# Constant products on TensorE in the waits of a token tower's block stages

## The reference

```python
h = _L0_tok_ref(x, ...)
h = h + _L0_attn_ref(_layernorm(h), ...)   # softmax attention over 64 tokens, a norm over the whole batch, relu
h = h + _L0_ffn_ref(_layernorm(h), ...)    # rmsnorm, 4-head attention with rotary tables, rmsnorm, 8 gated experts, 2 chosen
h = h + _L1_attn_ref(_layernorm(h), ...)   # norm, softmax attention with relative bias, norm
h = h + _L1_ffn_ref(_layernorm(h), ...)    # gelu hidden layer, softmax router, 1 of 8 experts
h = h + _L2_attn_ref(_layernorm(h), ...)   # linear attention with two softmaxes, norm, gelu mlp
h = h + _L2_ffn_ref(_layernorm(h), ...)    # shared mlp and 4 relu experts, 2 chosen
h = h + _L3_attn_ref(_layernorm(h), ...)   # sigmoid attention with 8 heads
h = h + _L3_ffn_ref(_layernorm(h), ...)    # top 2 of 8 gelu experts
```

## Time and profile before

| | us |
|---|---|
| median of three runs | 8839.58 (8835.07 to 8847.66) |
| the profiled execution, its own time | 8844.81 |
| its span, first to last instruction | 8843.0 |
| tokenizer, up to the load of the weights | 5853 |
| first loop (`l0a`), eight iterations | 5875 to 6073 |
| second loop (eight stages), eight iterations | 6100 to 8843 |

### The profile page before, as it was taken

One profiled execution on the slowest core, in us unless ns is written; L12 is line 12 of the kernel. 1 busy time (PEld: TensorE's weight loads), 2 busy tenths in 40 slices (PEclk: granted clock), 3 DMA queues, 4 the chain that ended last, 5 costly groups with the idle time before them and its releaser, 6 DMA issues. The chain is left out here.

```text
span 8843.0 us, 127696 instructions
## 1 busy us (share of the span) xinstructions
PE 7317.0 (83%) x40310; PEld 3642.9 (41%) x40310; DVE 5728.9 (65%) x11559; ACT 2224.5 (25%) x3750; POOL 31.1 (0%) x35
## 2 busy tenths in 40 slices
PE   6888886999999699999879999965666766767667
PEld 5544444544444644444452222223333333333333
DVE  4799995688888478888747777755454454454453
ACT  3222122211111211111132222223333333333333
POOL 0000000000000000000000000000000000000000
PEclk8999998999999899999989999976777777778788
DMA  7655557666666866666684444420000000000000
GB/s 214 136 126 121 126 126 182 193 178 180 181 181 181 219 170 181 181 180 179 169 218 118 122 123 118 117 83 5 1 2 3 1 3 3 1 3 3 1 3 2
DMA packets 641754, 957.80 MB, mean 108 GB/s; under 512 B 527640, under 2 KB 531296, under 8 KB 582758
## 3 DMA queue, kind: packets, MB, share of 16 engines
q1 hardware_dynamic: 641416, 953.52, 40.8%
HBM read 621.97 MB, written 344.28 MB: 109 GB/s over the span
## 5 line engine op out<-in xcount | busy, mean ns | idle before, releaser
L603 PE MATMUL abank<-inv_basis,mode_tile 128*128 128x512 f32 x2048 | 1023.9, 624 | 172.6 <-DMA mode_tile<-m_modes 161.8
L970 DVE TENSOR_TENSOR work<-inv_copy,abank 128x512 f32<-128x512 f32 x1024 | 657.2, 683 | 613.9 <-ACT inv_copy L845 613.5
L665 PEld LDWEIGHTS gbank<-fwd_basis,turned 128*128 128x128 f32 x6368 | 747.1, 193 | 369.8 <-issue 221.5
L665 PE MATMUL gbank<-fwd_basis,turned 128*128 128x128 f32 x6368 | 823.0, 283 | 51.3 <-ACT turned L853 51.3
L1001 DVE TENSOR_TENSOR arena<-zbank,work 128x512 f32<-128x512 f32 x1024 | 701.6, 685 | 207.5 <-PE zbank L638 207.4
L634 PE MATMUL zbank<-arena,conv_bd 128*64 128x512 f32 x3072 | 829.2, 618 | 3.1 <-DVE mixed L1159 2.2
L636 PE MATMUL zbank<-arena,conv_bd 128*64 128x504 f32 x3072 | 779.6, 586 | 0.0
L638 PE MATMUL zbank<-arena,conv_bd 128*64 128x504 f32 x3072 | 779.6, 586 | 0.0
L1003 DVE SCALAR_TENSOR_TENSOR arena<-arena 128x512 f32<-128x512 f32 x1024 | 708.5, 692 | 35.4
L853 ACT ACTIVATE turned<-tbank 128x512 f32<-128x512 f32 x796 | 432.0, 594 | 1100.5 <-PE tbank L652 1100.5
L603 PEld LDWEIGHTS abank<-inv_basis,mode_tile 128*128 128x128 f32 x2048 | 365.4, 196 | 543.6 <-issue 495.4
(11 more groups left out here) (302 smaller groups left out, 9180.3 us busy)
## 6 DMA issues: line engine op xcount, KB each, us to landing
h_rows<-arena SPq DMA_DIRECT2D x192, 1024.0 KB, 16.3
arena<-h_rows SPq DMA_DIRECT2D x192, 1024.0 KB, 6.2
arena<-h_rows SPq DMA_DIRECT2D x384, 496.0 KB, 8.9
m_modes<-mixed SPq DMA_DIRECT2D x64, 1024.0 KB, 6.7
mode_tile<-m_modes SPq DMA_DIRECT2D x512, 128.0 KB, 4.3
g_modes<-modes_out SPq DMA_DIRECT2D x192, 256.0 KB
arena<-x_slots SPq DMA_DIRECT2D x192, 194.9 KB
arena<-g_modes SPq DMA_DIRECT2D x36, 1024.0 KB, 11.0
```

The costliest lines, as they stand in the source:

```text
L603: last = nc.tensor.matmul(abank[px][:], mode_tile[u][:, 2 * px + k, :, :].rearrange("p a c -> p (a c)"), inv[:, 2 * px + k, :], start=True ...
L665: last = nc.tensor.matmul(gbank[u][:, 128 * k:128 * k + 128], turned[q][:, k // 2, k % 2, b, :], fwd[:, 2 * q + b, k, :], start=(q == 0 an ...
L970: nc.vector.tensor_tensor(inverse[:, 2 * k + part, :], inv_copy[k][:], abank[1][:], op)\
```

## The change

A helper `fill(n, bank)` issues n products of constants: stationary operand `cst[:, 0:128]`, moving operand `cst[:, 0:512]`, into a whole PSUM bank that is free at that place. No semaphore is counted by them and nobody reads the bank before it is written again. Thirteen places in TensorE's program call it, 11 products in each iteration of the first loop and 108 in each iteration of the second. Nothing is removed or moved.

```diff
+        def fill(n, bank):
+            for _ in range(n):
+                mm(bank[:], cst[:, 0:128], cst[:, 0:512])
...
 (attn_tensor, behind the scores, ahead of the softmax's transposes; l0a and l1a)
+            fill(11, B[0][1])
             p.need("dve", "p", 1)
...
         def l0b_tensor(p):
+            fill(3, B[0][1])
...
         def l0f_tensor(p):
+            fill(6, B[0][1])
             halves_tensor(p, "r", r, "r.out")
...
                     if k == 0:
+                        if u == 0:
+                            p.need("dve", "masked0", 0)
+                            fill(20, B[0][0])
                         p.need("dve", "p", u)
...
+            fill(4, B[0][2])
             halves_tensor(p, "f", r, "f.out")
...
+            fill(11, B[0][0])
             for u in R:
                 p.need("dve", "gates", u)
...
         def l1a_tensor(p):
+            fill(6, B[0][0])
...
         def l1f_tensor(p):
+            fill(16, B[0][1])
...
         def l2a_tensor(p):
+            fill(6, B[0][2])
...
+            fill(6, B[1][2])
             stacked_tensor(p, "f", "f.out")
...
         def l2f_tensor(p):
+            fill(7, B[0][0])
...
         def l3a_tensor(p):
+            fill(6, B[0][0])
...
         def l3f_tensor(p):
+            fill(6, B[0][0])
```

## The result

The changed kernel takes 8877.17 us (median of 6 runs, 8862.20 to 8898.57) against 8840.92 (6 runs, 8835.07 to 8850.27) of the kernel before: ratio 1.004, interval 1.0026 to 1.0054, or 36 us slower. The sign is as forecast, and the time lies in the range, but the loss is 36 us where 79 were forecast.

A forecast was written before the change was run, and what follows sets the result against it. The kernel was taken as bound by one chain passing between engines, none near full, with TensorE's clock low in waits. Lateness 26.5 plus slow starts 7.5 less faster work 26, with the first loop, gave +79 us: 8918, range 8825 to 9010.

The forecast's parts named there:

- The sign: Whole kernel: slower, forecast 0.9%; slower had chance 0.74, same 0.12, faster 0.14.
- term 3: Second loop: slow work between the waits becomes fast, 63 us of it at 0.41, saving 26 us per iteration.
- term 2: Second loop: fills that begin at the low clock lose 2.5 us at three places, 7.5 us per iteration.
- the line for `l0b`: Ahead of `l0b` in the second loop: fill of 2.6 us against a wait of 4.7, so not late.
- term 1: Second loop: fills longer than their waits make TensorE late, 26.5 us per iteration, none of it hidden.
- The price of a product: Every fill: one product is two records, 0.86 us at clock 1.00 and about 1.75 us at 0.50.
- rival D: All fills: a product costs a quarter of the rows' price, none is late; about 8615 us, chance 0.04.
- The sum: Second loop: 26.5 + 7.5 - 26 = +8 us per iteration, +64 in eight; with the first loop +79.
- The first loop's term: First loop: fill of 11 late by 3.7 us, about 1.8 given back; +1.9 per iteration, +15 in eight.
- Rival B: Second loop: clock high everywhere, no fill begins slow, 34 us of work saved; about 8780 us, chance 0.12.
- Rival C: Second loop: clock falls between fill and work, all twelve late fills begin slow; about 9095 us, chance 0.08.

The follow-up runs named there:

- no_head: The changed kernel without its fill of 3 products ahead of `l0b`, the other twelve fills as they are; 8882.88 us, 1.0048 of the kernel before.
- head_moved: The changed kernel with the 3 products ahead of `l0b` put at the end of `l3f`, in front of the loop's jump; 8888.61 us, 1.005 of the kernel before.
- fine: The changed kernel with products of 256 columns, their numbers fitted to the waits, none at `l0b`; 8652.08 us, 0.9784 of the kernel before.
- thin: The changed kernel with all fill products on 8 rows of the array instead of 128; 9724.34 us, 1.0998 of the kernel before.
- fit: The changed kernel with each full-width fill cut to the 0.86 us products that fit its wait, none at `l0b`; 8671.42 us, 0.98 of the kernel before.
- part runs: The kernel before with only the 20 products in the softmax of `l0f` (8897.08 us), or only the 47 at six openings behind `x_stacked` (8800.55 us).
- plus: The fitted full-width fills with one product more at every place, two at the softmax of `l0f`; 8686.33 us, 0.9826 of the kernel before.
- heated: The fitted full-width fills, 3 at the first norm of `l0f`, plus a few products in short waits where the clock still fell; 8649.59 us, 0.9781 of before.
- softmax_only: The kernel before with only the 20 products in the softmax of `l0f` added; 8897.08 us, 1.0058 of the kernel before.

## Why the prediction was right, and where not

The sign and the mechanism held: late fills cost about as much as the clock returns. The size did not, 36 us instead of 79. What failed are three terms of the second loop's sum: term 3, which counted 63 us of work that becomes fast where it was 85.4; term 2, 7.5 us where 2.6 came; and the line for `l0b` in term 1, "not late", which was late by 3.8.

**The price of a product: right.** 0.86 us at 1.00 and 1.75 at 0.50. Twelve records take 5.4 us (5.2 were forecast), none of such groups 2.6, and rival D fell with it.

**Term 1, +26.5 us: right.** The fills that run at 1.00 have the lengths forecast: 9.5 at the router and in `l1a`, 3.3 at the second norm, 5.0 at `l2a` and `l3f`, 13.6 at `l1f`.

**Term 2, +7.5 us: too large by 4.9.** The places where the wait is longer than term 1 makes it are the softmax of `l0f` (18.6 against 17.2), the start of `l1a` (6.6 against 5.2) and some fills of `l3a` (5.7 against 5.2 on average), together 3.4 us. Net of the fast fills, up to 0.2 us shorter than 0.86 times their number, it is 32.9 - 26.5 - 3.8 = 2.6 us. The first norm's fill, one of the three that I took as slow, isn't: it stands behind the three products of `l0b`, and no_head shows that they are the reason (5.2 us with them, 7.4 without). The clock that my step read from a row of the kernel before was changed by the fill ahead of it.

**`l0b`, "2.6 against 4.7, not late": this step failed.** It is late by 3.8 us. I compared a fast fill with the wait and saw in the wait only a wait for ScalarE. In the changed kernel's row TensorE begins 3.61 us after its last work, with no engine to wait for, and then works three products slowly. The same jump is there before too, under a wait for ScalarE that is longer than the pause:

```profile
6783.07 0.63 PE L1616 MATMUL banks<-constants,pT 128*128 128x128 f32 x4 [0.85 <-ACT pT L2761]
6788.33 1.27 PE L1816 MATMUL banks<-constants,qt 64*128 64x64 f32 x8 [4.63 <-ACT qt L1810]
```

That the jump is what takes the 3.6 us is argued from its place (it is there once in each iteration, and absent where a fill stands elsewhere); that it can be hidden by products queued ahead of it is shown by head_moved.

**Term 3, -26 us: too small by 4.9.** The work gained 30.9. The step took 81 us of slow time in the work before, left 18 of them slow, and priced the other 63 at 0.41. By the table the slow time in the work is 99.2 before and 13.8 after, so 85.4 us went, and they brought 30.9, 0.36 each. What was sized wrong is how many of them go, and most of that is the 81. I took nine tenths of the long waits as slow, 62 of 68.5 us, with the softmax wait of `l0f` as the only one read. By the trace of the kernel before it is 48.5: 2.5 of the 6.1 us at the softmax of `l1a`, 0.6 of the 4.5 at `l2f`. The slow time that isn't there lies in the work. Of the two stretches that I left slow, the sums of `l1f` became fast (the slow part of `l1f`'s work fell from 17.5 to 3.4) and the end of `l2f` stayed slow as I had it (17.6 to 7.5).

**The sum.** Together -4.9, -4.9 and +3.8: +2.0 us an iteration instead of +8, and 11 us in the whole second loop instead of 64. The first loop's term was right, 18 us for 15. That gives 29 us in place of 79. The profiled executions are only 17 apart because that of the changed kernel reached the first loop 11.6 us earlier, in code that is the same. The 7 us between 29 and the 36 of the medians are within the spread of the six runs, 36 us.

**Rival B** had half of the mechanism: the clock is 0.97, near to everywhere high. It was to save 34 us of work; 31 came. What it left out are `l0b` and the slow starts that remain, together 6.4 us, and those put the result on the slower side. The Trainium skill's advice against idle gaps between bursts of products ("TensorE: Matmul & The Clock Gate", section "Why this matters for your kernels") agrees with the traces as far as the clock goes, 0.79 to 0.97. It says nothing of what a filled gap may cost, and that decided the time here: 8877 us with the gaps overfilled, 8652 with the same gaps but that of `l0b` filled to their ends (fine).

**Rival C** fell: 13.5 of 101.4 us in fills and waits are slow.

**What is shown and what isn't.** Shown: the clock's return and the fills' lateness are two effects of about 31 and 33 us that cancel (thin has the second alone, fine has nearly the first alone). Shown too: the softmax of `l0f` loses and the openings win taken together. By place it is argued from the sums that the lateness decides. Open: why the clock stays low at the end of `l2f` in the changed kernel, what the pause in `l0f` is, what the places that didn't run alone are worth, and the spread between executions, in the unchanged code too.

## What to carry to other kernels

Work put into a wait to hold TensorE's clock has a price of its own, records times duration, and belongs sized against that wait alone; here overlong fills gave +0.4%, fitted ones (fit and fine) -2.0 and -2.2%, and fitted ones with a few more in short waits -2.4%. In the part runs fills 0.9 to 1.3 us too long got that back and more, and those 5.8 and 7.8 us too long didn't, the first of them with 42 us of work behind it. Ahead of a loop's jump, queue the products before the jump rather than behind it: behind it three of them cost 3.8 us, ahead of it nothing at that place. And before two profiled executions are subtracted, compare where the changed part begins in each.

## What the runs showed of the hardware

- In the changed kernel TensorE's first instruction behind the loop's jump comes 3.1 to 3.6 us after its last one ahead of it, with no engine to wait for; products queued ahead of the jump overlap with it (fill and wait together 5.2 us in head_moved, instead of 6.3).
- A product on 8 of 128 rows takes as long as one on all (1.73 us each at the clock it was granted), but leaves the clock at 0.73 though TensorE is busy nine tenths of the iteration (thin); full-height ones of the same number hold 0.97.
- In `l0f`, behind the softmax, TensorE pauses with no engine to wait for: in every iteration of fit and plus (1.0 to 1.7 us), heated and softmax_only (0.6 to 1.5). In the traces of the other ten kernels there is none above 0.4 us at that place. The row of fit's waits shows it as its longest; the cause is open.

```profile
PE banks L1645 <- issue: 16.7, 40, 1.5
```
